# Edge stage of a two-layer GNN: one matmul a subtile for the weight matrix, keyed by 12 destinations and 10 classes

## What is computed

```python
h = relu(layernorm(x))
# layer 1: messages, their sum by destination, node update
m = mish(mish(concat(h[src], h[dst], edge_attr) @ W1 + b1) @ W2 + b2)
agg = segment_sum(m, dst)
u = mish(concat(h, agg) @ W3 + b3) @ W4 + b4
x = x + layernorm(h + u) * gamma + beta
# layer 2: a low-rank convolution over the same edges, weighted
h = relu(layernorm(x))
S = (h @ U * s) @ Vt
x = x + relu(segment_sum(S[src] * edge_weight, dst) + bias)
```

## Time and profile before

| | |
|---|---|
| median of 3 runs | 1516.62 us (1515.47 to 1517.41) |
| profiled execution, first to last instruction | 1514.7 us |
| PE / DVE / ACT / POOL busy | 98% / 93% / 86% / 71% |
| granted TensorE clock, mean | 0.997 |
| DMA, mean | 135 GB/s |
| edge stage, first to last adjacency matmul | about 86 to 1383 us |

### The profile page before, as it was taken

The page is one execution under the profiler, slowest core; times in us unless marked ns, Lnnn a source line. Parts: engine busy times, 40 slices in busy tenths (PEclk is TensorE's granted clock), DMA queues, the critical chain, the costliest instruction groups (busy, mean ns, idle before and its releaser), DMA issues.

```text
span 1514.7 us, 33348 instructions
## 1 busy us (share of the span) xinstructions
PE 1490.6 (98%) x7862; PEld 1166.5 (77%) x7862; DVE 1413.2 (93%) x2920; ACT 1303.0 (86%) x2510; POOL 1077.3 (71%) x978
## 2 busy tenths in 40 slices
PE   7989999999999999999999999999999999999998
PEld 6766777777777777777777777777777777777885
DVE  7889999999999999999999999999999999996676
ACT  5088999999999999999999999999999999996562
POOL 1266888788788888878888887888878788863320
PEclk9999999999999999999999999999999999999999
DMA  8866555455555555555555555554555555554773
GB/s 292 271 218 171 120 124 119 114 127 123 119 118 125 118 117 127 122 119 118 125 118 117 124 124 120 118 125 118 116 125 124 120 118 125 118 128 100 175 167 148
DMA packets 124757, 205.10 MB, mean 135 GB/s; under 512 B 31642, under 2 KB 57370, under 8 KB 124721
## 3 DMA queue, kind: packets, MB, share of 16 engines
q0 software_dynamic: 58528, 112.91, 35.1%
q1 hardware_dynamic: 65840, 91.24, 19.5%
q10 hardware_dynamic: 352, 0.52, 0.1%
HBM read 151.60 MB, written 42.75 MB: 128 GB/s over the span
## 4 chain that ended last, share of the span: by engine, by line
PE 94%; DVE 3%; ACT 1%; DMA 1%; issue 1%; SPq 0%; POOL 0%; POOLq 0%; DVEq 0%; ACTq 0%
PE bm L1158 56%; PE bp L1137 7%; PE bp L1145 6%; PE bs L1181 5%; PE bp L1147 5%; PE pm L1169 2%; PE pu L336 2%; PE po L2146 2%; PE pu L2124 2%; PE pB L723 2%; PE pA L723 2%; PE pm L1168 2%; PE pu L2191 1%; DMA M_tab<-zero 1%; PE pu L2178 1%
## 5 line engine op out<-in xcount | busy, mean ns | idle before, releaser
L1062 POOL TENSOR_TENSOR hTl<-tp,hTh 128x512 fp32r<-128x512 f32 (+1 forms) x314 | 414.3, 1319 | 153.6 <-DVE khl L1357 152.8
L1158 PE MATMUL bm<-W2h,hTh 128*128 128x512 f32 x1252 | 499.4, 399 | 1.1 <-DVE bm L1350 0.5
L1158 PE MATMUL bm<-W2l,hTh 128*128 128x512 f32 x1252 | 497.1, 397 | 0.0
L1158 PE MATMUL bm<-W2h,hTl 128*128 128x512 f32 x1252 | 494.6, 395 | 0.0
L1049 POOL DMA_INDIRECT xg<-A_tab,idx x305 | 324.0, 1062 | 102.8 <-issue 79.7
L1158 PEld LDWEIGHTS bm<-W2h,hTh 128*128 128x128 f32 x1252 | 235.7, 188 | 73.3 <-DVE bm L1350 18.7
L1158 PEld LDWEIGHTS bm<-W2l,hTh 128*128 128x128 f32 x1252 | 235.5, 188 | 57.3
L1158 PEld LDWEIGHTS bm<-W2h,hTl 128*128 128x128 f32 x1252 | 235.6, 188 | 53.6
L1217 ACT ACTIVATE rp<-bp 128x512 f32<-128x512 f32 (+1 forms) x314 | 183.8, 586 | 100.4 <-PE bp L1147 98.9
L1321 DVE SCALAR_TENSOR_TENSOR rp<-rp 128x512 f32<-128x512 f32 (+1 forms) x314 | 214.8, 684 | 29.5 <-issue 13.4
L1331 DVE SCALAR_TENSOR_TENSOR tp<-rp,bp 128x512 f32<-128x512 f32 (+1 forms) x314 | 211.8, 675 | 7.6 <-POOL hTl L1062 2.8
(11 more groups left out here) (248 smaller groups left out, 2308.9 us busy)
## 6 DMA issues: line engine op xcount, KB each, us to landing
ea<-in_eaT SPq DMA_DIRECT2D x156, 128.0 KB
M_tab<-mev POOLq DMA_DIRECT2D x157, 80.0 KB, 6.3
agg_tab<-ev POOLq DMA_DIRECT2D x157, 64.0 KB, 2.5
db<-in_dst_rows SPq DMA_DIRECT2D x78, 128.0 KB
M<-M SPq DMA_DIRECT2D x76, 128.0 KB
M_tab<-zero SPq DMA_DIRECT2D x10, 640.0 KB
xg<-A_tab,idx POOLq DMA_INDIRECT x313
eaW<-Bh_tab SPq DMA_DIRECT2D x77, 64.0 KB
```

Source lines behind the costliest of these rows:

```text
L1062: e.tensor_tensor(hTl[p][:, j, 0:w], pick(u, start_t, tp)[:, 0:w], hTh[p][:, j, 0:w], ALU.subtract)\
L1158: last = e.matmul(bank[0:r, :], a[p][:, c, j * P:j * P + r], w[:, c, :], start=False, stop=c == KC - 1 and w is W2l, skip_group_check=True)
```

## The change

The matrix gets 10 classes of 128 columns and windows of 12 destinations, so 120 keys. The key's one-hot becomes bare (`key`, 120 wide), and the column's one-hot carries the two parts of the weight (`so`, 2 x 128). One matmul of 256 columns a subtile then gives both products side by side in `pm`, and they have to be added when they are copied out: ScalarE copies the high ones to `mev` (now ahead of its 1237) and a new operation on VectorE, `join`, adds the low ones from `pm`. `join` stands between VectorE's 1321 and 1337 at j = 0. TensorE's first adjacency matmul of the next group and POOL's store wait for `join` (`s_mev`) rather than for ScalarE's copy (`a_adj`). Left out of the diff below: the semaphore `s_prep` is split in two, `s_ea` for the cast 1297, for which the copies of line 962 wait, and `s_hot` for the one-hot 1304; and the prologue's spare tile `room` grows from 80 to 112 columns.

```diff
-EQ = 8
+EQ = 10
-EWIN = 16
+EWIN = 12
...
-        so = [sb(f"so{i}", [P, EC], F32R) for i in range(2)]
-        khl = [sb(f"khl{i}", [P, 2, KEYS], F32R) for i in range(2)]
+        so = [sb(f"so{i}", [P, 2, EC], F32R) for i in range(2)]
+        key = [sb(f"key{i}", [P, KEYS], F32R) for i in range(2)]
...
+        def matrix(u, low):
+
+            n = 1 if tail(u) else SUB // HSUB
+            of = pm[0:KEYS, 0:n * 2 * EC].rearrange("p (h a n) -> p h a n", h=n, a=2)[:, :, low, :]
+            return mev[u.par][:, 0:n * EC].rearrange("p (h n) -> p h n", h=n), of
...
                 if half == 0:
-                    e.wait_ge(a_adj, u.group(1, 1))
+                    e.wait_ge(s_mev, u.group(1, 1))
...
-                i, r, half = u.const % 2, ETAIL if tail(u) else P, pm[:, u.j // HSUB * EC:(u.j // HSUB + 1) * EC]
+                i, r, o = u.const % 2, ETAIL if tail(u) else P, u.j // HSUB * 2 * EC
                 if u.j == 0:
-                    wait(e, a_adj, u.group())
+                    wait(e, s_mev, u.group())
                 e.wait_ge(v_adj, u.val(2, 2))
-                e.matmul(half, khl[i][0:r, 0, :], so[i][0:r, :], start=u.j % HSUB == 0, stop=False, skip_group_check=True)
-                e.matmul(half, khl[i][0:r, 1, :], so[i][0:r, :], start=False, stop=u.j % HSUB == HSUB - 1 or tail(u),
-                         skip_group_check=True).then_inc(s_adj, 1)
+                e.matmul(pm[0:KEYS, o:o + 2 * EC], key[i][0:r, :], so[i][0:r, :, :].rearrange("p a n -> p (a n)"),
+                         start=u.j % HSUB == 0, stop=u.j % HSUB == HSUB - 1 or tail(u), skip_group_check=True)\
+                 .then_inc(s_adj, 1)
...
                 e.wait_ge(s_adj, u.val(1, 1 if tail(u) else SUB))
                 wait(e, q_adj, u.group(32, -32))
-                n = EC if tail(u) else 2 * EC
-                e.activation(mev[u.par][:, 0:n], pm[:, 0:n], ACT.Copy).then_inc(a_adj, 1)
+                to, of = matrix(u, 0)
+                e.activation(to, of, ACT.Copy).then_inc(a_adj, 1)
...
                     if pre and u.has(PRES):
                         pre_chain(u, k)
+                    if pre and k == 0 and g.j == 0 and g.has(MSGS):
+                        adjacency(g)
                     if not pre and m.has(MSGS):
                         msg_chain(m, k)
-                    if not pre and k == 0 and g.j == 0 and g.has(MSGS):
-                        adjacency(g)
...
-                e.tensor_scalar(so[i][0:r, :], iota_q[0:r, :], scol8[0:r, c], None, ALU.is_equal).then_inc(v_adj, 1)
-                e.scalar_tensor_tensor(khl[i][0:r, :, :],
-                                       iota_k[0:r, :].rearrange("p (a k) -> p a k", a=1).to_broadcast([r, 2, KEYS]),
-                                       kcol[0:r, c],
-                                       wcol_hl[0:r, c, :].rearrange("p a (h k) -> p (a h) k", k=1).bitcast(F32)
-                                       .to_broadcast([r, 2, KEYS]), ALU.is_equal, ALU.mult).then_inc(v_adj, 1)
+                e.tensor_scalar(key[i][0:r, :], iota_k[0:r, :], kcol[0:r, c], None, ALU.is_equal).then_inc(v_adj, 1)
+                e.scalar_tensor_tensor(so[i][0:r, :, :],
+                                       iota_q[0:r, :].rearrange("p (a n) -> p a n", a=1).to_broadcast([r, 2, EC]),
+                                       scol8[0:r, c],
+                                       wcol_hl[0:r, c, :].rearrange("p a (h n) -> p (a h) n", n=1).bitcast(F32)
+                                       .to_broadcast([r, 2, EC]), ALU.is_equal, ALU.mult).then_inc(v_adj, 1)
+
+            def join(u):
+
+                e.wait_ge(a_adj, u.group(1, 1))
+                to, of = matrix(u, 1)
+                e.tensor_tensor(to, of, to, ALU.add).then_inc(s_mev, 1)
...
             def step(s):
-                u, m, v, f = s + DVE_PRE, s + -DVE_MSG, s + PRE_AHEAD, s + -(DVE_MSG + 1)
+                u, m, v, f, a = s + DVE_PRE, s + -DVE_MSG, s + PRE_AHEAD, s + -(DVE_MSG + 1), s + -ADJ_EV_LAG
                 if u.has(PRES):
                     pre(u, 0)
                 if v.has(PRES):
                     square(v)
+                if a.j == 0 and a.has(MSGS):
+                    join(a)
                 if u.has(PRES):
                     pre(u, 1)
```

More of the change, by code:

```diff
@@ L409, in gnn_two_layers @@
             tb = [sb1(f"tb{i}", [P, H]) for i in range(TB)]
-            sb1("room", [P, 80])
+            sb1("room", [P, 112])
             tbh = [sb1(f"tbh{i}", [P, H], F32R) for i in range(TB)]
@@ L899, in edge_narrow @@
         s_go = sem("e_go")
-        s_prep = sem("e_prep")
+        s_ea = sem("s_ea")
+        s_hot = sem("e_hot")
         s_oh = sem("e_oh")
@@ L917, in edge_narrow @@
         a_adj = sem("a_adj")
+        s_mev = sem("e_mev")
         q_adj = sem("e_adjq")
@@ L992, in window_copy @@
             def window_copy(u):
-                e.wait_ge(s_prep, u.group(2, 1))
+                e.wait_ge(s_ea, u.group(1, 1))
                 copy(e, u.par, ETAIL if tail(u) else G)
@@ L1204, in _ @@
             e.wait_ge(v_msg, MSGS)
-            e.wait_ge(a_adj, NG)
+            e.wait_ge(s_mev, NG)
         @work.on("scalar")
@@ L1272, in _ @@
             b = [e.value_load(base_i[0:1, 3 * g:3 * g + 1], min_val=0, max_val=NP - WIN) for g in range(2)]
-            e.wait_ge(s_prep, 1)
+            e.wait_ge(s_ea, 1)
             copy(e, 0, G)
-            e.wait_ge(s_prep, 3)
+            e.wait_ge(s_ea, 2)
             copy(e, 1, G)
@@ L1296, in prep @@
                     wait(e, s_pre, u.val(1, -4))
-                    e.tensor_copy(M2[p][:, 0:n], ea[p][:, 0:n]).then_inc(s_prep, 1)
+                    e.tensor_copy(M2[p][:, 0:n], ea[p][:, 0:n]).then_inc(s_ea, 1)
                 elif k == 2:
-                    e.wait_ge(s_prep, u.group(2, 1))
+                    e.wait_ge(s_ea, u.group(1, 1))
                     e.tensor_tensor(M2[p][0:64, 0:n], ea[p][0:64, 0:n], M2[p][0:64, 0:n], ALU.subtract)\
@@ L1304, in prep @@
                     e.tensor_scalar(M1[p][0:64, 0:n], db[p][:, 0:n], base_b[0:64, gs, 0], iota_p[0:64, :],
-                                    ALU.subtract, ALU.is_equal).then_inc(s_prep, 1)
+                                    ALU.subtract, ALU.is_equal).then_inc(s_hot, 1)
             def onehot(u):
```

## The result

The changed kernel takes 1519.73 us (median of 11 runs, 1518.47 to 1521.25), the one before beside it 1516.19 (11 runs, 1514.69 to 1518.65): a ratio of 1.0023, 95% interval 1.0014 to 1.0031. It is slower, by 3.5 us; the forecast, 1536, stood 19.4 above the kernel before.

The account below looks back on a forecast made before the run. TensorE bounds the kernel, held through a loop by VectorE's bias copy. `join` 0.33 less compare 0.02 less TensorE 0.06 gave 0.25 a group, +19.3 over 77 groups, startup +0.4: 1536 us, range 1518 to 1549.

Parts of the forecast that it names:

- the loop: TensorE 1147 of step 4g-1, ScalarE's step, VectorE 1321 to 1350, TensorE's messages of step 4g+1; delay moves TensorE one for one.
- step 4g: The one-subtile step, once per four-subtile group, copying out the previous group's weight matrix; its bias copy would be 0.31 later.
- VectorE's prices: `join` adds 0.33 us a group (0.2 to 0.57); the narrower plain compare saves 0.02 a subtile (0 to 0.05).
- The rival in which `join` is held as 1372 is: Slower still: gaps around `join` on VectorE add 0.24 us a group, +18.5, giving 1555; chance 0.08.
- ScalarE, the two waits for `join`: Early copy-out and later message chain cost nothing; TensorE's first adjacency matmul has 0.9 us cover, POOL's store wait costs 0.
- The clearing stores: At startup, same bytes in 1024-byte instead of 1280-byte pieces: 0.4 us once, up to 2.7 by number of pieces.
- TensorE, per subtile: 0.03 saved: Two 160-column adjacency matmuls become one of 256: 0.18 or 0.19 out, 0.16 in; bounds 0 and 0.07.
- a turn to the transposes: On TensorE behind the second adjacency matmul: 0.04 of its 0.11 us, expected to stay after the change.
- the return part: Two subtiles between TensorE's stall and the next loop's 1147; only savings there count, forecast 0.06 us a group.
- The sum: Bias copy 0.31 later less 0.06 on TensorE: net 0.25 a group, +19.3 over 77 groups, startup +0.4.
- What would show it: 1158's load wait for 1350 grows from 14.1 to some 35 us, always in step 4g+1; groups last 16.8.
- The rival "even": Low ends together: `join` 0.2, compare 0.05 less, TensorE 0.07 a subtile; 0.01 a group, 1518; chance 0.06.

Follow-up runs that it names:

- runs 1 and 2: 1: changed kernel without `join`, low part not added, 1494.62 us; 2: kernel before plus the same addition to an unused tile and early copy-out, 1542.36 us.
- run 7: Kernel before with the second adjacency matmul, the low part of the weights, left out: 1497.79 us, ratio 0.9879.
- runs 5 and 6: 32 spare bytes in SBUF behind the edge weights; 5: in the kernel before, 1509.14 us; 6: in the changed kernel, 1527.24 us.
- run 3: Changed kernel with the 256-column adjacency matmul split into two of 128, same weights: 1530.21 us, ratio 1.0094.

## Why the prediction was wrong

- **What bounds the kernel, and the loop**: right. The bias copy of step 4g was the loop's last link and moved TensorE one for one (runs 1 and 2).
- **VectorE's prices**: right. `join` 0.33, measured 0.334; the compare 0.02, measured 0.02. The rival in which `join` is held as 1372 is did not occur. By the Trainium skill's rule on two Vector instructions with no wait between them ("VectorE: DVE Perf Modes"), 1372 is held and `join` is not. The trace agrees: the cast starts 0.334 behind `join` in the mean, as the sum had it without a gap.
- **ScalarE, the two waits for `join`**: hidden, as forecast. Nothing of them is among the waits of the changed kernel's TensorE. The clearing stores, forecast at 0.4 us once, landed in 10.72 us where they took 10.62, and POOL's first store waited 7.75 where it waited 7.39.
- **TensorE, per subtile: 0.03 saved**: this step failed, as a price and with its bound of 0.07. It took the second matmul's 0.11 as 0.07 and a turn to the transposes of 0.04 that would stay. There is no turn (run 7): the 0.11 was the second matmul's own, and the four transposes behind it were longer with it as well, by 0.02 in run 7 and by 0.03 in the changed kernel. The saving was 0.098: 0.066 without a turn (0.074 + 0.112 out, 0.120 in), and 0.032 on the transposes. In the return part that is 2 x 0.098 = 0.20 a group in place of 0.06, some 11 us over 77 groups.
- **What was left out**: the place of the tiles. The two subtiles of the return part hold 24 message matmuls, 24 x 0.004 = 0.10 us a group, 7 us measured (runs 5 and 6; which moved tile does it is argued). It isn't part of what the change does, and the prediction costed the shorter constants at nothing without saying so.
- **The sum**: +0.31 on the loop, -0.20 and -0.10 in the return part: +0.01, where the forecast had +0.25. Groups became 0.05 longer and the kernel 3.5 us slower. At equal places the same sum gives 0.31 - 0.20 = +0.11, and 0.15 was measured (16.48 to 16.63, and 16.57 to 16.73); the 0.04 that are left I did not place (run 3 has the like: 0.19 put back, 0.14 seen). So the change itself costs 10.6 to 11.3 us, over half of the forecast, and the moved tiles hid most of that.
- **What would show it**: the wait for the bias copy was to grow from 14.1 to some 35 us and became 56.5, on the loads alone. That was the sign of TensorE's error: it arrived about 0.25 us earlier than I had it (0.20 + 0.10 in place of 0.06), not VectorE later.
- **The rival "even"** took the same mechanism at its low ends, with 0.07 a subtile and `join` at 0.2. The time came near it (1518), and so just inside the forecast's range (1518 to 1549), by luck: `join` and the compare cost what the forecast took and not their low ends, TensorE saved more than the low end's 0.07, and 7 us came from the moved tiles.

## What to carry to other kernels

When a step leaves a busy queue, price it by what the whole stretch loses, its neighbours included, and set the upper bound above its own rows: here these gave 0.07, and 0.098 were saved. Compare the places of the operands, modulo 64 bytes here, before a difference of half a per cent is put down to an edit: a spare tile of 32 bytes in both kernels tells. And where two engines share work on one step, look for which operations fall beside POOL's before the order is changed; the order that kept POOL beside PSUM work made this change pay, at 1492.8 us, and two that didn't cost 44 and 152.

## What the runs showed of the hardware

- Message matmuls of 512 columns in fp32r follow each other in 229 to 230 ns where their stationary tiles begin on a multiple of 64 bytes of a partition, and in 233 to 234 where these begin 32 behind one (nine kernels and four; 32 spare bytes turned it both ways). Other tiles moved along with them.
- A second matmul of 160 columns with its load, between a matmul of 512 and four transposes, costs some 130 ns; 96 columns more on a single one cost some 35; two of 128 columns cost as much as two of 160 (0.51 us for the stretch).
- VectorE's compare of 120 columns, 0.27 us, becomes 0.94 beside POOL's subtraction of 512 columns, and a one-hot of 128 columns, 0.28 alone, becomes 1.00; copies into PSUM and products with a PSUM operand aren't changed by it.
